# A two-layer gated cross-attention kernel: layer 0's scores taken from two-head stacks, half of the heads in each 64 partitions, with the row products placed between the other half's score products

## What is computed

```python
# x: (16, 56, 128), ctx_1024: (16, 1500, 128), mask: (16, 1, 56, 1500); 16 heads of 8
q = einsum('nqhd,od->nqho', layernorm(x) by heads, Wq); k, v likewise from ctx_1024
energy = einsum('nqhd,nkhd->nhqk', q, k)
energy = where(mask == 0, -1e20, energy)
attn = softmax(energy / sqrt(128), axis=3)
out = einsum('nhqk,nkhd->nqhd', attn, v) @ Wo.T + bo
x = x + tanh(g_xattn[0]) * out
```

## Time and profile before

| | before |
|---|---|
| median of three runs | 1247.59 us |
| the profiled execution | 1246.21 us, of which its span 1244.5 us |
| PE busy | 1132.7 us (91%) |
| DVE busy | 884.8 us (71%) |
| ACT busy | 699.7 us (56%) |
| POOL busy | 516.2 us (41%) |
| mean granted TensorE clock | 0.971 of full speed |

### The profile page before, as it was taken

One profiled execution on the slowest core, in us unless ns is written; L12 is line 12 of the kernel. 1 busy time (PEld: TensorE's weight loads), 2 busy tenths in 40 slices (PEclk: granted clock), 3 DMA queues, 4 the chain that ended last, 5 costly groups with the idle time before them and its releaser, 6 DMA issues.

```text
span 1244.5 us, 27943 instructions
## 1 busy us (share of the span) xinstructions
PE 1132.7 (91%) x10056; PEld 647.0 (52%) x10056; DVE 884.8 (71%) x1242; ACT 699.7 (56%) x967; POOL 516.2 (41%) x352
## 2 busy tenths in 40 slices
PE   4689999999999989778879999999999999999984
PEld 2255656666565646533434555555555555555542
DVE  7766666666666664587787768768676867877668
ACT  2355555555555536445566656666565656666542
POOL 8546666666666743433212322322232223223210
PEclk9899999999999989699998999999999999999996
DMA  3456565455554462000006786666675676666520
GB/s 106 124 169 202 163 185 155 150 156 159 179 157 150 133 154 66 1 1 25 1 18 129 148 144 132 144 136 150 124 145 116 146 149 127 144 135 151 112 62 15
DMA packets 222263, 151.29 MB, mean 122 GB/s; under 512 B 184576, under 2 KB 195312, under 8 KB 222208
## 3 DMA queue, kind: packets, MB, share of 16 engines
q1 hardware_dynamic: 221920, 150.56, 50.0%
q10 hardware_dynamic: 288, 0.00, 0.0%
HBM read 62.23 MB, written 25.39 MB: 70 GB/s over the span
## 4 chain that ended last, share of the span: by engine, by line
PE 77%; DVE 11%; issue 6%; ACT 5%; POOL 0%; ACTq 0%; DVEq 0%; POOLq 0%
PE bank L880 17%; PE bank L898 16%; PE bank L755 8%; PE bank L848 6%; PE bank L779 6%; PE bank L783 5%; PE bank L796 5%; DVE region L1702 2%; PE bank L856 2%; DVE e_row L1520 2%; ACT region L1228 2%; PE bank L920 2%; PE bank L1121 2%; PE bank L826 2%; PE bank L1083 2%
## 5 line engine op out<-in xcount | busy, mean ns | idle before, releaser
L1520 DVE CUSTOM_DVE_ANT_0 e_row<-bank,region 112x1500 f32<-112x1500 f32 x128 | 220.1, 1720 | 124.8 <-PE bank L755 123.6
L1228 ACT ACTIVATE region<-bank 125x896 f32<-125x896 f32 x192 | 176.0, 917 | 203.0 <-PE bank L783 203.0
L1559 DVE TENSOR_REDUCE neg_max<-bank 128x1 f32<-128x1500 f32 x112 | 192.7, 1721 | 130.9 <-PE bank L880 130.8
L880 PE MATMUL bank<-region 128*128 128x500 f16 x1008 | 235.5, 379 | 3.3 <-ACT e_row L1255 1.8
L1264 ACT COPY region<-bank 128x768 f16<-128x768 f16 x224 | 178.0, 794 | 88.3 <-PE bank L848 88.3
L1255 ACT ACTIVATE e_row<-bank,neg_shift 128x1500 f32<-128x1500 f32 x112 | 169.3, 1511 | 68.8 <-DVE neg_shift L1563 38.6
L573 POOL CAST u_w<-e_row 128x1500 f16<-128x1500 f32 x56 | 80.6, 1439 | 215.2 <-ACT e_row L1255 215.2
L573 POOL CAST wg_sb<-e_row 128x1500 f16<-128x1500 f32 x56 | 81.8, 1461 | 199.0 <-ACT e_row L1255 154.9
L880 PEld LDWEIGHTS bank<-region 128*128 (+1 forms) x1008 | 97.3, 98 | 108.1 <-issue 3.7
L779 PE MATMUL bank<-row_of,region 112*128 112x448 bf16 x384 | 137.7, 359 | 7.6 <-ACT region L1228 7.6
L783 PE MATMUL bank<-region 97*128 (+1 forms) x768 | 137.6, 260 | 0.0
(11 more groups left out here) (218 smaller groups left out, 1517.6 us busy)
## 6 DMA issues: line engine op xcount, KB each, us to landing
region<-region SPq DMA_DIRECT2D x192, 96.0 KB, 2.2
turned_rows<-region SPq DMA_DIRECT2D x16, 768.0 KB, 3.8
region<-turned_rows SPq DMA_DIRECT2D x32, 384.0 KB, 3.5
c_in<-in_ctx SPq DMA_DIRECT2D x16, 750.0 KB
split_rows<-region SPq DMA_DIRECT2D x16, 750.0 KB
region<-in_mask_Bx1xSxS_if SPq DMA_DIRECT2D x32, 328.1 KB
region<-split_rows SPq DMA_DIRECT2D x24, 250.0 KB
g_w<-split_rows SPq DMA_DIRECT2D x24, 250.0 KB
```

Of the source, the lines that this page charges most:

```text
L880: last = pe.matmul(score_banks1(par, t)[:, k, :], q1[:, ql, b, 128 * t:128 * (t + 1)], c_t1[par][:, cl, 4 * k:4 * k + 4, 0:KP], start=(ql ...
L1228: act.activation(p0[:, 2 * i:2 * i + 2, :], ring0("s", h, i)[0:KP, :, 0:HALF_ROWS], ACT.Exp, scale=SCALE0)\
L1520: dve.tensor_tensor_reduce(out=masked.rearrange("p (a k) -> p a k", a=3), in0=bank[0:R0, 0:3, 0:4 * KP], in1=mask_bias[par][:].rearrange(" ...
L1559: dve.tensor_reduce(neg_max[:, t:t + 1], score_banks1(par, t), AX.XY, ALU.max, negate=True)\
```

## The change

- A stack now holds two heads instead of four: high, low, the row of maxima at partition 32, and high again, 49 partitions. Heads 0 to 7 lie from partition 0, heads 8 to 15 from partition 64. A chunk needs four products of 112 columns (L798) instead of two of 224.
- The row products of half 1 - h lie in the other 64 partitions than the scores of half h, and stand between them: one 500-column product (L765) after the first mask product, one amid the scores, one after the second mask product.
- `mask_bias`, `row_of` and `ident16` are used in 56 partitions of either half.
- DVE takes the maxima in two parts (banks 0 and 1, then bank 2), and joins them in `dve_neg0`.
- `sync_stack` reads `turned_rows` back from DRAM, in pieces of 16 partitions x 4 pairs of heads x 1536 numbers (192 KB), six of them, and copies the batch's queries into `q_now` (two transfers of 49 partitions). It waits until `turned_rows` of that batch has been written.
- The contexts are turned a batch earlier on PE's clock: `pe_prep0(b + 2)` stands in half 1 of batch b, and SP issues in batch b: stack b + 1, context b + 2, mask b + 2, `split_rows` b + 2, `turned_rows` b + 2. POOL makes `split0(b + 2)` right after `mask0(b + 1)`.
- Steps 0 and 1 of the values move to the end of the half before.

```diff
-        RING0 = [("s", 0, 0), ("prep", 0), ("s", 0, 1), ("spread", 0), ("s", 0, 2), ("prep", 1), ("s", 0, 3), ("s", 0, 4),
-                 ("s", 0, 5), ("neg", 0), ("s", 1, 0), ("s", 1, 1), ("spread", 1), ("s", 1, 2), ("s", 1, 3), ("s", 1, 4),
-                 ("s", 1, 5), ("neg", 1)]
+        RING0 = [("s", 0, 0), ("s", 0, 1), ("spread", 0), ("s", 0, 2), ("s", 0, 3), ("s", 0, 4), ("s", 0, 5), ("neg", 0),
+                 ("s", 1, 0), ("s", 1, 1), ("prep", 0), ("spread", 1), ("s", 1, 2), ("s", 1, 3), ("prep", 1),
+                 ("s", 1, 4), ("s", 1, 5), ("neg", 1)]
+        ROWS_AT = (0, 1, 3, 4)
...
             wait_apart(sp, "sp", (sem("st0"), (b - 1) * (2 * NP)))
-            for n in range(2):
-                wait_apart(sp, "sp", (sem(f"ct_done0_{n}"), b + 1))
-                for g in range(G):
-                    for at in ((0, 64), (32,))[n]:
-                        sp.dma_start(c_stack[par][at:at + 32, g], c_t0[32 * g:32 * g + 32, n])\
-                            .then_inc(sem(f"stack{par}_{g}"), 16)
+            wait_apart(sp, "sp", (sem("turned_out0"), 16 * (b + 1)))
+            turned = turned_rows[b].rearrange("(g p) n c k -> p n g (c k)", p=2 * D0)
+            for half in range(2):
+                for at, n in ((0, 0), (2 * D0, 1), (33, 0)):
+                    sp.dma_start(c_stack[par][64 * half + at:64 * half + at + 2 * D0].rearrange("p g c k -> p g (c k)"),
+                                 turned[:, n, 4 * half:4 * half + 4]).then_inc(sem(f"stack{par}_{half}"), 16)
+                if isinstance(b, int) and b == 0:
+                    sp.wait_ge(sem("q0_low"), 2 * H)
+                low = slice(64 * half, 64 * half + KS)
+                sp.dma_start(q_now[par][low].rearrange("p g o s -> p (g o s)"),
+                             q0[low, b].rearrange("p g o s -> p (g o s)")).then_inc(sem(f"stack{par}_{half}"), 16)
...
-                    sync_split_out(sp, b + 1)
+                    sync_stack(sp, b + 1, 1 - par)
                     if not (isinstance(b, int) and b + 2 >= B):
                         sync_load_context(sp, b + 2, par)
-                    sync_stack(sp, b + 1, 1 - par)
-                    sync_turned_out(sp, b + 1)
-                    if not (isinstance(b, int) and b + 2 >= B):
                         sync_load_mask(sp, b + 2)
+                        sync_split_out(sp, b + 2)
+                        sync_turned_out(sp, b + 2)
...
+            def masks(n):
                 c = 2 * i + n
-                into = ring0("s", h, i)[:, n, :]
-                pe.matmul(into[:, 0:HALF_ROWS], mask_flat[par][:, KP * c:KP * c + 128], row_of[:].rearrange("p h s -> p (h s)"),
-                          start=True, stop=False)
-                for g in range(2):
-                    rows = HALF_ROWS * h + GC * g
-                    last = pe.matmul(into[:, GC * g:GC * (g + 1)], c_stack[par][0:97, 2 * h + g, c, :],
-                                     q0[0:97, b, rows:rows + GC], start=False, stop=(g == 1))
-            last.then_inc(sem("st0"), 1)
+                pe.matmul(into[:, n, 0:HALF_ROWS], mask_flat[par][low:low + S, KP * c:KP * c + 128],
+                          row_of[low:low + S].rearrange("p h s -> p (h s)"), start=True, stop=False)
+
+            def scores(n, pairs):
+                for g in pairs:
+                    last = pe.matmul(into[:, n, R0 * g:R0 * (g + 1)].rearrange("p (o s) -> p o s", o=2),
+                                     c_stack[par][low:low + KS, g, 2 * i + n, :], q_now[par][low:low + KS, g, :, 0:S],
+                                     start=False, stop=(g == 3))
+                return last
...
+            masks(0)
+            beside(0)
+            scores(0, (0, 1))
+            beside(1)
+            scores(0, (2, 3))
+            masks(1)
+            beside(2)
+            scores(1, range(4)).then_inc(sem("st0"), 1)
...
+                        if i in (1, 3) and h == 1 and not (isinstance(b, int) and b + 2 >= B):
+                            wait_ring0(pe, b, par, "prep", i // 2)
+                            pe_prep0(pe, b + 2, i // 2, ring0("prep", i // 2))
...
+            for part, (a, z) in enumerate(((0, 2), (2, 3))):
+                wait_apart(dve, "dve", (sem("scores0"), 2 * (b * T0 + t) + (part + 1)))
+                dve.tensor_tensor_reduce(out=masked[:, 4 * KP * a:4 * KP * z].rearrange("p (a k) -> p a k", a=z - a),
```

More of the change, by code:

```diff
@@ L51, in flamingo_kernel @@
     MASKED = 1e19
+    RT = 64 + S
+    KS = 33 + 2 * D0
+    HP = H // 2
     T1 = ROWS // 128
@@ L961, in layer0 @@
                                 pe_proj0(pe, b - 1, ring0("spread", h))
[L962 to L967 removed]
+                    pe_pv0(pe, b, par, h, 0)
                     if has_after:
@@ L975, in _ @@
             pe_spread0(pe, B - 1, 0, ring0("spread", 0))
-            for i in range(NP):
+            for i in range(2, NP):
                 pe_pv0(pe, B - 1, 1, 1, i)
@@ L1278, in act_context0 @@
                 act.wait_ge(sem("turned_out0"), 16 * b)
-                for g in range(G):
-                    act.wait_ge(sem(f"stack{1 - par}_{g}"), per_use(b - 1, 1 - par, 48))
             act.copy(c_t0[:, n].rearrange("p c k -> p (c k)"),
@@ L1637, in layer0 @@
                     has_after = h == 0 or not last
-                    if has_after:
-                        dve_max0(dve, after[0], after[1], 4 * after[2] + 1)
-                    if not first:
-                        dve_inv0(dve, b - 1, h, ring0("spread", h))
-                    if has_after:
-                        for t in (2, 3):
-                            dve_max0(dve, after[0], after[1], 4 * after[2] + t)
+                    for t in range(4):
+                        if has_after:
+                            dve_max0(dve, after[0], after[1], 4 * after[2] + t)
+                        if t == 1 and not first:
+                            dve_inv0(dve, b - 1, h, ring0("spread", h))
+                    if has_after:
                         dve_neg0(dve, *after, ring0("neg", h))
-                    if not last:
-                        dve_max0(dve, b + 1, 1 - par, 4 * h)
             batches(dve, layer0)
```

237 lines of the change are left out of this document (124 added, 113 removed).

## The result

The changed kernel takes 1439.51 us (median of 4 runs, 1438.1 to 1441.97) where the kernel before takes 1247.61 beside it: a ratio of 1.154, with a 95% interval of 1.152 to 1.156. The forecast was 1400 with a range of 1290 to 1425. The sign and most of the size came as forecast, and the time lies 14.5 us above the range.

What follows compares the result with a forecast made beforehand. PE was taken to bound the kernel at 26.5 us a batch; a transfer chain of 36.4 adds 139 us, and the start 6, 5 and 2: +152 on 1246.2, so 1398 profiled, 1400 median, range 1290 to 1425.

Steps and rivals of the forecast that it cites:

- What bounds the kernel before: Layer 0's loop: PE, busy 91% of the span, sets the pace at 26.5 us a batch, with DVE close behind.
- The gain on PE: Row products beside the other half's scores: some 5.4 us a batch off PE, +0.8 for weight loads, about 22 left.
- 12 to 13.5 us a half: DVE's half with two maxima instructions a tile: about 10 us of work, the rest waits.
- The ring's legs: Write 3.9, stack and context 18.5, POOL's split 4.8, PE and ACT 8.8, semaphores 0.4: 36.4 us a batch.
- The rate of the 16-partition pieces: Stack transfers taken at a halved rate, 115 GB/s, so 10.3 us; 1360 to 1425 us given 0.60.
- So I add 1.4: Leg from turn to next write: 7.4 us at full clock, 8.8 with PE's clock lowered by some 9 us idle.
- Batches 14 and 15 ... stay near 26 us: 0: The last two batches of layer 0 have no turn, so they add nothing to the time.
- Without any transfer in the way a batch would last 24 to 27 us: PE and DVE in the new order, with no transfer late, against 26.5 us a batch before.
- the ring: Write, stack, context, split and turn each wait for the one before: +9.9 us a batch, +139 over batches 0 to 13.
- The rivals: Stack at old rate 1307 (0.20), as issued 1293 (0.06), faster (0.07), no change (0.03), row products not beside scores 1410.
- The one on the other side: Row products vanish from PE and nothing else waits: 22 to 24 us a batch, 1175 to 1207; faster given 0.07.
- The signs: Period 35 to 38 us, PE's longest waits at the turns, stack at some 110 GB/s, low clock in part of every batch.

Runs made afterwards that it cites:

- e16_fill: e13_compute_alone plus 22 discarded PE products a batch where PE would wait for DVE: 1389.87 us (ratio 1.101 to 1.116).
- e13_compute_alone: Changed kernel with next to no stack from batch 2 on, the context issued ahead of it, and POOL's mask made behind `negc`: 1336.8 us (two runs).
- e4_mask_behind: Changed kernel with only POOL's mask made to wait until DVE has made `negc` of the first half: 1432.85 us (ratio 1.142 to 1.155).
- e14_hold_alone: e13_compute_alone with POOL's mask made where the changed kernel makes it: 1428.85 us (ratio 1.142 to 1.146).
- e18_before_late: Kernel before the change, with DVE clearing a scratch row (1.4 us) ahead of half 0's `negc` once a batch: 1271.31 us, ratio 1.018.
- e7_context_mask_wider: Changed kernel with context ahead of stack, mask behind `negc`, and each stack half's first two pieces as one of 32 partitions: 1368.07 us.
- e8_warm: Changed kernel with the mask behind `negc` and twenty discarded PE products ahead of the first turn: 1467.83 us (ratio 1.175 to 1.181).
- e17_fill_real: e7_context_mask_wider plus the discarded products of e16_fill and twelve more ahead of half 0's first row products: 1433.39 us (ratio 1.145 to 1.150).

## Why the prediction was wrong, point by point

- **What bounds the kernel before**: nothing in the runs speaks against PE at 91%, at a clock of 1.00 from 64 to 460 us.
- **The gain on PE**: the row products do run beside the other half's scores (317.02 and 317.03 are the starts of a mask and of a row product in the changed kernel). At full clock the gain shows: PE is busy 78.31 / 3 = 26.1 us a batch in the stretch of e16_fill, of which the 22 idle products are some 4.2 by their expectation's estimate. That leaves about 22, as forecast, against 376.77 x 26.5 / 396 = 25.2 before. That PE would "wait elsewhere anyway" held too.
- **DVE**: I had 12 to 13.5 us a half. In e13_compute_alone, at a clock of 1.00, a half lasted from 305.65 to 319.56, 13.9 us. Of that, 1.4 are the join of the maxima and `negc` held by POOL's split; the rest is what I had.
- **The ring's legs**: forecast 3.9, 18.5, 4.8, 8.8 and 0.4; measured 3.6, 19.4, 4.7 and 10.3. The rate of the 16-partition pieces, the most uncertain term, was right: 121 GB/s from 312 to 314, for 115. By the Trainium skill, SBUF — State Buffer, Door 1: The DMA port swizzle, 16 partitions reach 104 GB/s and 32 twice as many ports; the traces agree in the ratio, and lie above the figure, with 121 to 130 for 16 and 234 for 32.
- **The step that failed in the sum: "So I add 1.4".** I let the lower clock touch one leg only, because PE "will have stood idle for some 9 us each time" and the clock had come back within 2 us near the start. Here it doesn't come back: PE was busy all of 318 to 327 at 0.50, over layer 0 the clock is 0.68, and PE idles 3.87 us at the turn, not 9. The last leg took 10.3 for 8.8 + 0.4, with the twelve products of a turn at 1.46, where they take 0.83 before the change. Rounds of 38.2 for 36.4 are +25 us, less the 5 counted apart for the weight loads. About 1.1 of the 1.8 us a round are this leg; most of the rest is the stack and the context, 19.4 for 18.5.
- **"Batches 14 and 15 ... stay near 26 us: 0", and the start.** After the last write, at 610.59, the last two batches took about 31 us each (from the last stack's issue at 614.01 to the last scores at 676.0), at a low clock for part of the time and with one more hold, at 612.98. The first copy of `any_row` came 7.2 us late for the 2 forecast. These give some 15 of the remaining 20 of the 40 us.
- **The step that failed in the mechanism: "Without any transfer in the way a batch would last 24 to 27 us".** This was the assumption behind every rival, and it is wrong by more than any other: 32.4 us with the clock as it falls (e13_compute_alone), 28.1 with the clock held up (e16_fill, batches 2 to 4). Therefore the ring, though it is there and about as long as forecast, was not what made the kernel slower by itself. It stood beside two other causes, and cutting it gave 13 us. That a sum of the ring alone came within 40 us is in part luck: the ring without the mask's hold has a period of 38.3 us (e4_mask_behind), and the hold without the ring one of 38.4 (e14_hold_alone).
- **The rivals**: none had DVE held by POOL. The one on the other side, 22 to 24 us a batch, is excluded by e13_compute_alone.
- **The signs**: the turns were to be PE's longest waits, once a batch. They were not; PE waited twice as long for `negc`. The other signs came, the period of 38.8 just above the 35 to 38 named.

The causes, by what their removal gave: ring alone 13 us, hold alone 7, both 47, both and the wider pieces 71, both and no stack 103. Some 89 are left then, 95 in the profiled run. There the 13 middle batches of e13_compute_alone last 31.5 us, for 26.2 before. The batches of e16_fill at a clock of 1.00 last 27.9 to 28.9, so that about 3 of these 5.3 us are the clock and some 2 are the waits between PE and DVE, or the products that filled them: by this estimate 42 and 27 us. Another 17 are the first interval, 43.2 us for 26.1, with PE's wait of 9.0 for a stack that was still whole.

Left open: why the changed mix loses the clock to its waits, where the old one kept it through a wait of 1.4 us in every batch. Two differences are at hand. Its waits come in groups (1.03, 0.29, 1.32, 0.25 and 1.09 us within 15 us of e13_compute_alone, one of 1.4 in e18_before_late), and its scores use 49 and 56 rows of the array, where the old ones used 97 and 112. No run told these apart. Nor did a run show a version that beats the kernel before: the best that computes the whole is e7_context_mask_wider, 1368.

## What to carry to other kernels

When a cause has been found in a trace, ask what the time would be without it, and make the kernel that shows it. A ring, a held instruction and a slow clock hid one another here: taking away the ring or the hold alone gave 13 and 7 us of 192. A PE that is 100% busy in a slice may be busy at half speed: read the granted clock beside every busy share, and cost a change that trades PE's work for short waits of PE at both of the clock's levels.

## What the runs showed of the hardware

- A DVE instruction of 0.16 us with two inputs in SBUF lasted 5.23 to 5.28 when POOL's mask (6.5 us, from and to SBUF) had begun 0.06 to 0.09 us ahead of it, and 0.15 when it began 0.06 us ahead of the mask (271.10 and 271.16). So the order of the starts, within 0.1 us, decided over 5 us. The Trainium skill, SBUF — State Buffer, SBUF: two separate sides, says that the two engines share a pair of ports as a lock, held for a whole instruction by the one that starts first. The changed kernel agrees on who is held, but the held instruction ended 1.2 us before the mask did. e18_before_late doesn't agree: there `negc`, with the same two inputs, began 1.05 us into the mask, behind a DVE memset, and took 0.10 us. No run shows why.
- PE's clock fell behind waits of about 1 us that came close together (e13_compute_alone), and behind the hold of 5 us (0.53 from 351 to 352 in the changed kernel). In the changed kernel it then stayed at 1.2 GHz for up to 27 us, half of the times for 10 to 14, also with PE busy throughout. The Trainium skill, TensorE: Matmul & The Clock Gate, A second HAM failure mode: psum-queue depth-cycling, tells of the same in another kernel, short idle times between groups of products that let the clock oscillate; it gives no price, and here it was some 5 us a batch in batches 2 to 4 (33.0 for 28.1).
- Twenty or 22 products more a batch, in a loop of two batches' code, made PE stop for 4.0 to 5.1 us in five turns of the loop (e8_warm, e16_fill, e17_fill_real). A filler on an engine with a long loop isn't free even where the engine idles.
